# First attention stage of a two-block vision kernel: the second relative-position table goes out on GpSimd's queue

## The reference

```python
attn = jnp.einsum('bqc,bkc->bqk', q * scale, k)
rel_h = jnp.einsum('bhwc,hkc->bhwk', r_q, Rh)
rel_w = jnp.einsum('bhwc,wkc->bhwk', r_q, Rw)
attn = (attn.reshape(-1, WS, WS, WS, WS) + rel_h[:, :, :, :, None] + rel_w[:, :, :, None, :]).reshape(-1, N, N)
attn = jax.nn.softmax(attn, axis=-1)
out = jnp.einsum('bqk,bkc->bqc', attn, v)
```

## Time and profile before

| | before |
|---|---|
| median of 3 runs | 886.08 us (885.78 to 888.82) |
| the profiled execution | 884.12 us |
| its span | 882.3 us |
| PE busy | 789.6 us, 89% |
| DVE busy | 513.7 us, 58% |
| ACT busy | 433.0 us, 49% |
| POOL busy | 143.4 us, 16% |

### The profile page before, as it was taken

The page is one execution under the profiler, slowest core; times in us unless marked ns, Lnnn a source line. Parts: engine busy times, 40 slices in busy tenths (PEclk is TensorE's granted clock), DMA queues, the critical chain, the costliest instruction groups (busy, mean ns, idle before and its releaser), DMA issues.

```text
span 882.3 us, 20283 instructions
## 1 busy us (share of the span) xinstructions
PE 789.6 (89%) x6794; PEld 644.7 (73%) x6794; DVE 513.7 (58%) x1516; ACT 433.0 (49%) x1419; POOL 143.4 (16%) x293
## 2 busy tenths in 40 slices
PE   3688798897988887789998999999999999997998
PEld 2566576675756654589986888888888888876998
DVE  5156657667576677455525475756575666674542
ACT  1035445556465565454424465555555555554432
POOL 8310111102011110032221011010101010100211
PEclk9569889999899999799996999999999999999999
DMA  6482010100101010100030303030303030300001
GB/s 94 99 197 41 6 35 9 28 21 16 27 7 34 11 26 2 36 1 1 0 57 17 58 16 70 5 74 1 74 0 71 0 71 1 74 1 1 19 18 36
DMA packets 39950, 29.89 MB, mean 34 GB/s; under 512 B 13382, under 2 KB 38038, under 8 KB 39872
## 3 DMA queue, kind: packets, MB, share of 16 engines
q1 hardware_dynamic: 36518, 26.16, 14.0%
q0 software_dynamic: 2544, 2.35, 1.6%
q10 hardware_dynamic: 810, 0.40, 0.3%
HBM read 8.79 MB, written 1.57 MB: 12 GB/s over the span
## 4 chain that ended last, share of the span: by engine, by line
PE 70%; SPq 11%; DVE 7%; issue 4%; POOL 3%; DMA 2%; ACT 2%; DVEq 0%; POOLq 0%; ACTq 0%
PE bank L1236 10%; PE bank L1315 8%; PE bank L495 7%; PE bank L474 7%; SPq L1129 6%; PE bank L1263 5%; PE bank L1243 5%; PE bank L1282 4%; PE bank L1104 3%; PE bank L920 3%; PE bank L1343 3%; PE bank L937 3%; PE bank L1375 3%; PE bank L1038 2%; SPq L1593 2%
## 5 line engine op out<-in xcount | busy, mean ns | idle before, releaser
L666 ACT ACTIVATE Pb<-bank,nmax 128x256 f32<-128x256 f32 (+1 forms) x432 | 192.3, 453 | 95.7 <-DVE nmax L656 93.0
L656 DVE TENSOR_REDUCE nmax<-bank 128x2 f32<-128x392 f32 (+2 forms) x240 | 139.0, 580 | 51.1 <-PE bank L1236 30.2
L677 DVE TENSOR_SCALAR Pb<-Pb,rsum 128x196 f32<-128x196 f32 (+2 forms) x432 | 133.7, 347 | 8.5
L696 ACT COPY area<-bank 98x392 f32<-98x392 f32 (+1 forms) x144 | 77.4, 539 | 82.9 <-PE bank L1243 71.0
L1236 PE MATMUL bank<-K,Q 80*128 80x256 f32 x384 | 107.4, 405 | 5.5 <-DMA Q<-rel_dense 5.5
L1236 PEld LDWEIGHTS bank<-K,Q 80*128 80x128 f32 x384 | 69.4, 198 | 25.2 <-issue 14.5
L666 ACT ACTIVATION_READ_ACCUMULATOR Pb<-bank,nmax 128x1 f32 x432 | 87.4, 202 | 0.0
L937 PE MATMUL bank<-ident,Pb 128*98 128x128 f32 x384 | 65.2, 296 | 22.7 <-DVE Pb L677 22.7
L484 ACT ACTIVATE area<-bank,fc1b 128x256 f32<-128x256 f32 x96 | 45.2, 475 | 66.0 <-PE bank L474 64.8
L937 PEld LDWEIGHTS bank<-ident,Pb 128*98 128x98 f32 x384 | 42.3, 135 | 37.4 <-DVE Pb L677 17.6
L495 PE MATMUL bank<-fc2w,area 128*128 128x192 f32 x384 | 64.7, 326 | 0.0
(11 more groups left out here) (143 smaller groups left out, 1542.2 us busy)
## 6 DMA issues: line engine op xcount, KB each, us to landing
Q<-dense_q SPq DMA_DIRECT2D x16, 288.0 KB, 4.7
K<-dense_k SPq DMA_DIRECT2D x16, 288.0 KB, 6.7
operands<-dense_q SPq DMA_DIRECT2D x48, 32.0 KB, 2.0
operands<-dense_k SPq DMA_DIRECT2D x48, 32.0 KB, 2.0
Q<-rel_dense SPq DMA_DIRECT2D x32, 48.0 KB, 2.6
Q<-rel_dense POOLq DMA_DIRECT2D x32, 48.0 KB, 2.4
out<-x_all SPq DMA_DIRECT2D x8, 192.0 KB, 2.0
operands<-dense_q SPq DMA_DIRECT2D x45, 28.0 KB
```

Source lines behind the costliest of these rows:

```text
L656: nc.vector.tensor_reduce(nmax[0:sc.shape[0], u % 3, 0:sc.shape[1]], sc, AX.X, ALU.max, negate=True).then_inc(self.m_rdy, 1)
L666: nc.scalar.activation(Pb[u % 3][0:rows, t, 0:cols], sc[:, t, :], ACT.Exp, bias=nmax[0:rows, u % 3, t:t + 1], accum_out=esum[0:rows, u % 3 ...
L677: nc.vector.tensor_scalar(Pb[u % 3][0:rows, t, 0:keep], Pb[u % 3][0:rows, t, 0:keep], rsum[0:rows, u % 3, t:t + 1], None, ALU.mult).then_i ...
L696: copy(*self.pt_views(u)).then_inc(self.pt[self.pt_engine(u)], 1)
```

## The change

Table 1's transfers move from SP's queue (and ACT's, in image 0) to GpSimd's, with a semaphore of their own, `relscat_w`. SP sends table 0's six as soon as DVE has copied it, and no longer waits for ACT's copy of table 1. In `pool_front` GpSimd waits for ACT's copy, issues six transfers, and only then goes on to the wait for `scat` and the gathers. In image 0, SP and ACT send three transfers of table 0 each, and ACT waits for DVE's copy alone. PE waits for both semaphores.

```diff
@@ emit_scores
-                    eng.wait_ge(self.relscat, n.at(16 * 2 * GH0, 16 * 2 * GH0))
+                    eng.wait_ge(self.relscat, n.at(16 * GH0, 16 * GH0))
+                    eng.wait_ge(self.relscat_w, n.at(16 * GH0, 16 * GH0))
@@ act_rel
-                if n.counts(16 * 2 * GH0, 0):
-                    eng.wait_ge(self.relscat, n.at(16 * 2 * GH0, 0))
+                if n.counts(16 * GH0, 0):
+                    eng.wait_ge(self.relscat_w, n.at(16 * GH0, 0))
@@ scatter_rel
-            def scatter_rel(self, eng, p, heads):
+            def scatter_rel(self, eng, p, heads, tables):
                 for h in heads:
-                    for i in range(2):
+                    for i in tables:
                         at = 64 * (h % 2) + D0 + i * WS
                         eng.dma_start(Q0[p][at:at + WS, h // 2:NPAIR:GH0 // 2, :],
-                                      self.reld[i][h * WS:(h + 1) * WS, :, :]).then_inc(self.relscat, 16)
+                                      self.reld[i][h * WS:(h + 1) * WS, :, :])\
+                           .then_inc((self.relscat, self.relscat_w)[i], 16)
@@ sp
                     eng.wait_ge(self.g_out[1], n.at(5, 4))
                     land(eng, "sp")
-                    eng.wait_ge(self.g_out[0], n.at(6, 4))
-                    land(eng, "sp")
-                    self.scatter_rel(eng, p, range(GH0 // 2) if n.index0() else range(GH0))
+                    self.scatter_rel(eng, p, range(GH0 // 2) if n.index0() else range(GH0), (0,))
@@ pool_front
                 gather(xr0[:, :, :], xnT[:, :, :], self.xgath)
-                eng.wait_ge(self.scat, n.at(16 * 2 * GH0, 16 * 2 * GH0))
                 if n.counts(self.NU, -self.NU):
                     eng.wait_ge(self.s_rdy, n.at(self.NU, -self.NU))
+                eng.wait_ge(self.g_out[0], n.at(6, 4))
+                land(eng, "pool")
+                self.scatter_rel(eng, p, range(GH0), (1,))
+                eng.wait_ge(self.scat, n.at(16 * 2 * GH0, 16 * 2 * GH0))
                 land(eng, "pool")
@@
-                eng.wait_ge(self.relscat, n.at(16 * 2 * GH0, 16 * 2 * GH0))
+                eng.wait_ge(self.relscat, n.at(16 * GH0, 16 * GH0))
+                land(eng, "pool")
+                eng.wait_ge(self.relscat_w, n.at(16 * GH0, 16 * GH0))
                 land(eng, "pool")
@@ scatter_first (ACT, image 0)
-                act.wait_ge(a0.g_out[0], 4)
                 act.wait_ge(a0.g_out[1], 4)
-                a0.scatter_rel(act, 0, range(GH0 // 2, GH0))
+                a0.scatter_rel(act, 0, range(GH0 // 2, GH0), (0,))
```

More of the change, by code:

```diff
@@ L1109, in dve_rel @@
                 eng.wait_ge(self.g_rdy[1], n.at(5, 4))
-                if n.counts(16 * 2 * GH0, 0):
-                    eng.wait_ge(self.relscat, n.at(16 * 2 * GH0, 0))
+                if n.counts(16 * GH0, 0):
+                    eng.wait_ge(self.relscat, n.at(16 * GH0, 0))
                 m = GH0 * WS
@@ L1199, in setup @@
                 self.gath = sem("a0_gather")
+                self.relscat_w = sem("a0_relscat_w")
                 self.xmain = [sem("a0_xm0"), sem("a0_xm1")]
```

## The result

The changed kernel takes 878.63 us (median of 12 runs, 872.88 to 883.91) beside 885.97 us (12 runs, 883.82 to 889.23) for the kernel before on the same chip: ratio 0.9917, 95% interval 0.9894 to 0.9940. That is 7.3 us faster, with an interval of 5.3 to 9.4. The forecast was 4.6 us faster, or 881.5 us with a range of 877 to 886.5. The range holds the measured 878.63, but the forecast lies outside the interval, and the measured time lies in the window of a rival, *Costs hidden* (877.8 to 879.1, chance 0.22).

A forecast was written before the change was run, and what follows sets the result against it. The prediction took PE to be waiting on the issue rate of SP's queue in attention 0. Its terms, -5.1 - 1.9 + 1.0 + 1.4 = -4.6 us, took the median from 886.08 to 881.5 us, range 877 to 886.5.

The forecast's parts named there:

- Costs hidden: Rival: constants not delayed and scalings miss GpSimd's issues, so no costs; 877.8 to 879.1 us, chance 0.22.
- Image 1: Attention 0, image 1: PE's 4.03 us wait for table 1 goes, plus about 1 for the clock; 5.1 us gained.
- Later images: Attention 0 after image 1: shorter waits for table 1 and the gather gain 1.9 us, bounds 0 to 3.2.
- The prediction's own sign of being wrong: Wrong if image 0's first scores come over 2 us later, or an undisturbed image's 37.70 us period does not fall.
- Step 3: Image 0's head: the earlier large input transfer delays GpSimd's constants and attention 0; cost 1.0 us, bounds 0 to 3.4.
- Step 4: Attention 0, line 677: GpSimd's issues hold DVE's scalings, 0.2 us in each of seven images; cost 1.4 us, bounds 0 to 2.8.
- No wait for a table transfer in any image: Expected sign in the changed profile: line 920, the main scores, waits for no table transfer in any image.

The follow-up runs named there:

- e3: The changed kernel, but image 0's table transfers go out from SP and ACT as in the kernel before: 881.98 us beside 888.05, ratio 0.9923.
- e6: The changed kernel, but SP holds its large input transfer until GpSimd's constants have landed: 880.85 us beside 890.03, ratio 0.9897.
- e1: The kernel before, with SP sending table 0 as soon as DVE has copied it, nothing moved to GpSimd: 887.10 us beside 888.05, ratio 1.0005.
- e2: The kernel before, with 13 small weight transfers sent behind image 1's rows, nothing moved to GpSimd: 879.80 us beside 888.05, ratio 0.9915.
- e8: The changed kernel without the early start: SP waits for both copies before sending table 0. 880.29 us beside 890.03, ratio 0.9890.
- e7: The changed kernel, with the 13 small weight transfers also sent behind image 1's rows: 879.90 us beside 890.03, ratio 0.9888.
- e9: The changed kernel run once more, unaltered, as a yardstick: 879.81 us beside 888.06 for the kernel before, ratio 0.9921.
- e4: The changed kernel, with each of GpSimd's six table transfers cut into two halves in every image: 882.37 us beside 888.05, ratio 0.9963.
- e5: The changed kernel, with GpSimd's table transfers cut into halves from image 1 on only: 883.59 us beside 890.03, ratio 0.9920.
- e10: A repeat of e5, GpSimd's transfers halved from image 1 on in the changed kernel: 881.16 us beside 888.06, ratio 0.9949.
- e12: The changed kernel, with the last image's `xbias` of the last MLP on DVE instead of GpSimd: 879.55 us beside 885.94, ratio 0.9911.
- e11: The changed kernel without the early start, with 13 small weight transfers behind image 1's rows: 881.14 us beside 888.06, ratio 0.9918.

## Why the prediction was right, and what it missed

The direction and the range held, and the mechanism was the one named: SP's queue was late in image 1 by the rate of its issues. The forecast of -4.6 lies just outside the measured interval on the small side, and the sum behind it came near partly by luck, as the terms show. Of the rivals, *Costs hidden* came nearest: its time window holds the result, and its half on the scalings came true. Term by term:

**Image 1, -5.1.** The pair of traces shows -4.6; over the nine profiles with GpSimd's train other than e3 and e6, the period is 36.9 to 37.6 us, 37.2 in the middle, which is 5.0 less than 42.22. Right. It was put down to the wait and its clock. e1, e2 and e8 bear the wait out in the times: the early start alone leaves most of the gain away, and both ways of making SP earlier bring it. The period of about 37 us shows only in the kernels with the split; e2's image 1 takes 40.93. The clock's part shows in more rows than the prediction had: behind the waits of 4.03 us (before), 1.61 (e2) and 1.70 (e6) in image 1, and of 1.79 and 1.22 (e1) in images 2 and 4, the granted clock fell to 0.50 within 2 us of PE's resuming or during the wait. e1 and e3 have such a fall in image 1 without a wait (75.7 and 76.5 us), so not every one is a wait's doing.

**Later images, -1.9.** Images 2 to 6 lose 2.3 us, image 7 and the rest give 1.2 back, so the pair shows -1.1. Each of these stretches moves by 1 to 2 us with the place of the low-clock stretches (192.1 us in e2, 192.0 in e7, 191.1 in e9). Within the bounds; no better number than the bounds came out. The prediction's own sign of being wrong, that the undisturbed period of 37.70 us does not fall, did not come: the same image takes 37.34 us in the change and 37.60 in e9, a small fall.

**Step 3, the head, +1.0.** The input transfer went out at 32.83 as worked out (near 32.7). The `xr` gather moved from 39.45 to 40.70. Over all profiles it is a shift inside a scatter: with the input transfer at 32.8 to 33.2 us (the change, e4, e5, e7, e9, e10, e12) it stands at 38.85 to 40.95, in the mean 40.3; with a later one (36.5 to 36.6 in e1, e8 and e11, 39.1 to 39.2 in before, e2, e3 and e6) at 38.27 to 40.20, in the mean 39.2. The difference is 1.1 us with an error of about 0.4. So the 1.0 taken was a fair size for the gather. The first scores, which were to slip with it, stand 0.1 us earlier in the pair of traces. e6 shows another side, which the prediction did not have: with the transfer held, SP's last table-0 transfer of image 1 goes out 1.2 us later.

**Step 4, DVE held by GpSimd's issues, +1.4.** This is the step that failed. The prediction read the earlier trace rows as "a scaling from SBUF to SBUF can be held to the end of the GpSimd instruction in progress", and priced 0.2 us an image. The scalings inside the trains are not held: in the change 14 of line 677's shape of 128x196 meet an issue in attention 0 and take 321 ns in the mean, where those that meet nothing take 319, and one of them takes 365. Twice as many issues (e5, e10) leave attention 0 no longer. The shape's mean between 64 and 330 us does rise, from 325 ns to 329 in the change and 337 in e5 and e10, but by what stood beside the train: the gathers and `xbias` meet more scalings. PE's idle time ahead of the transposes of `Pb` (line 937, now 938) is 23.3 us where it was 22.7. In the earlier trace rows too the pair of 1.72 us ran on with the `xbias` operation of 508.23. The row at 7.77 is one issue of 2.77 us, of a transfer of 284.8 KB; it shows an issue holding a scaling, and which issues do is open. The cost of step 4 was about 0.

The Trainium skill (SBUF — State Buffer, "SBUF: two separate sides") says that DVE's perf-mode operations and GpSimd's operations exclude each other, and that the writing of descriptors is shut out by it too. The first half agrees with 508.23 and with e10's 0.74 us beside a gather. The second half, on issues of this size, doesn't: DVE's scalings are not longer inside the train by more than the 2 ns above, and the train itself is no longer, 3.42 us for six issues in image 1, where scalings lie in it, against 3.57 in image 0. The prediction had found that rule not to matter for the sum, and that held.

**What was missed, +1.5.** The closing drain of GpSimd. Its length goes with the transfers that GpSimd issued in the whole program:

| kernel | GpSimd's transfers | drain, us | DVE's last end to the end, us |
|---|---|---|---|
| before, e1, e2 | 37 | 4.14 | 2.58 |
| e3 | 79 | 7.16 | 3.61 |
| change, e6 to e9, e11 | 85 | 7.65 | 4.10 |
| e5, e10 | 127 | 11.08 | 7.53 |
| e4 | 133 | 11.57 | 8.02 |
| e12 | 85, done earlier | 7.67 | 2.58 |

From 79 transfers on it is 0.082 us for each, whatever their size: e4's and e5's carry half the bytes. The change adds 48 and pays 1.5 us in the trace, since the first 2 us of the longer drain are hidden beside the last output. No view of engine time shows it, since a drain is not counted as busy; it was there to be read in line 128 of the trace before, 4.14 us against PE's 3.12 and DVE's 0.60.

So -4.6 = -5.1 - 1.9 + 1.0 + 1.4 stands, in the pair of traces, against -4.6 (image 1) - 1.1 (later images) - 2.0 (clock between the first scores and image 1) - 0.1 (head) - 0.1 (behind) + 1.5 (drain) = -6.4, or -6.5 before rounding. A too pessimistic step 4 (1.4) and a missed drain (1.5) cancel, and so, nearly, do the too large gains of the images (0.5 and 0.8) and the too large cost at the head (1.1). That is luck. What is left of the difference is the clock at the head, which the change did not bring. But this is one pair: at equal clock it differs by about 4.5 us, and the means of the runs by 6.1, so 1.5 us of what the runs gained stand in no term here.

Some smaller readings were wrong. SP does not get to image 1 any sooner (71.42 against 71.56), as it has its issues behind the large transfer to get rid of at their own pace. "No wait for a table transfer in any image" is missed by 0.7 us. An issue of table 1 took GpSimd 0.56 us and not line 1433's 0.52, and that line's landing times are those of SP's transfers and GpSimd's together. And the bounds given for the costs and the later gain add up to 877.8 to 887.2 us, not to the "879 to 885" that is named with them.

**Open.** Why e3 spends 41.6 us in image 1 without a wait for a transfer: a stretch of low clock falls into it (76.5 to 83.3 us), and nothing here says why there. The size of the later images' gain, what the early start is worth, and why e12 is not faster in the times.

## What to carry to other kernels

When PE waits for the last of a row of equal transfers, look at the issuing queue before the bandwidth: here twelve issues of 0.8 us were the wait, and what cured it was either half of them on an idle queue or 13 unrelated small transfers sent later, each as good as the other and not both. Do both halves of such a change separately: one carried most of the gain. And before transfers are moved to GpSimd, look at how the program ends: every transfer that it ever issued lengthens its closing drain, which is free only if GpSimd finishes its last work some us before everyone else.

## What the runs showed of the hardware that was not expected

- GpSimd's closing drain grows with the transfers it has issued: 4.14 us with 37, 7.16 with 79, 11.57 with 133, from 79 on by 0.082 us for each. It starts when GpSimd's last wait is over.
- A transfer of 28 KB of the same shape takes GpSimd less to issue than SP: line 1130 in the changed kernel, ns min/median/max.

```profile
L1130 POOL DMA_DIRECT2D operands<-dense_k x48: 558/558/756, 41.4 to 306.1; - x48
L1130 SPq DMA_DIRECT2D operands<-dense_q x45: 807/807/921, 30.1 to 306.3; - x45
```

  Halves of it cost GpSimd 6.19 / 12 = 0.52 us each, nearly as much as a whole one.
- The granted clock falls, for 7 us and more, even while PE is busy all through. Some stand in one trace only, like that of the kernel before at 117 us. Others return at the same place of the program: ten of the fourteen profiles have one that starts 12.1 to 12.8 us behind image 5's first `q`/`k` product, in the kernel before at 234 us, and neither e1 nor a kernel with the doubled train has it. In these windows of the kernel before PE's busy time is the number right behind the length, and the clock, 0.55 and 0.53, the third from the end.

```profile
117.00:124.00 7.00, 7.00 (x45) 5.47 (x44) 3.82 (x14) 2.89 (x12) 1.49 (x6) 0.55 0.16 37
234.00:241.00 7.00, 7.00 (x36) 5.39 (x35) 3.14 (x10) 3.58 (x13) 1.57 (x6) 0.53 0.13 30
```
